# Dummy products of ones at the head of TensorE's program in seven stages of a transformer kernel

## What is computed

```python
x = x + attention0(layernorm(x), ctx, tau, delta)   # softmax attention, 16 heads of 16
x = x + moe0(layernorm(x))        # top 2 of 8 experts, 256-512-256, inner norm + GELU, outer norm
x = x + attention1(layernorm(x), ctx, tau, delta)
x = x + quantum_ffn(layernorm(x)) # 256-1024-256, hidden + c * sin(theta + hidden / 10), relu
x = x + window_attention(ctx, layernorm(x), len, p) # one head, masked, tanh of a projection
x = x + moe2(layernorm(x))        # top 2 of 8 experts, 256-1024-256, GELU
x = x + attention3(layernorm(x), ctx, tau, delta)
x = x + ternary_ffn(layernorm(x)) # rounded activations, weights in {-1, 0, 1}, silu(gate) * up
```

## Time and profile before

| | us |
|---|---|
| median of 3 runs | 2499.39 |
| lowest, highest | 2496.64, 2502.64 |
| profiled execution | 2496.09 |
| its span, first to last instruction | 2494.3 |
| mean granted clock of TensorE, share of full | 0.879 |
| first 40th to last: TensorE's granted clock in tenths | 9997559999955799899989655999999996999699 |

### The profile page before, as it was taken

The page is one execution under the profiler, slowest core; times in us unless marked ns, Lnnn a source line. Parts: engine busy times, 40 slices in busy tenths (PEclk is TensorE's granted clock), DMA queues, the critical chain, the costliest instruction groups (busy, mean ns, idle before and its releaser), DMA issues. The chain is left out here.

```text
span 2494.3 us, 40430 instructions
## 1 busy us (share of the span) xinstructions
PE 1960.8 (79%) x11858; PEld 1467.3 (59%) x11859; DVE 1378.0 (55%) x3378; ACT 894.4 (36%) x1938; POOL 522.7 (21%) x560
## 2 busy tenths in 40 slices
PE   6997419999800699699979751999999994999587
PEld 4665406666500366366666441899999993565255
DVE  5875426666467477778756443222222222787787
ACT  3452104444311344333312110333333332545587
POOL 1212532211187111101100164000000004562000
PEclk9997559999955799899989655999999996999699
DMA  6000231221121400000000323111111113110001
GB/s 243 1 1 22 80 132 57 63 62 61 56 74 58 180 1 1 13 1 0 0 8 10 135 89 108 30 38 34 38 35 36 38 34 121 39 47 1 8 27 35
DMA packets 81874, 125.70 MB, mean 50 GB/s; under 512 B 17104, under 2 KB 65872, under 8 KB 78704
## 3 DMA queue, kind: packets, MB, share of 16 engines
q1 hardware_dynamic: 46640, 68.02, 8.2%
q0 software_dynamic: 13104, 35.80, 4.4%
q10 hardware_dynamic: 22032, 20.62, 2.4%
HBM read 82.58 MB, written 41.81 MB: 50 GB/s over the span
## 5 line engine op out<-in xcount | busy, mean ns | idle before, releaser
L1386 ACT ACTIVATE e_hT<-psum,e_bt 128x128 f32<-128x128 f32 x568 | 154.2, 383 | 335.3 <-PE psum L1349 335.3
L1349 PEld LDWEIGHTS psum<-e_xT,e_w 128*128 128x128 f32 x2272 | 267.0, 193 | 8.4 <-ACT e_xT L1379 4.9
L1349 PE MATMUL psum<-e_xT,e_w 128*128 128x128 f32 x2272 | 267.7, 276 | 4.2 <-ACT e_xT L1379 4.2
L1358 PE MATMUL psum<-m_w,e_hT 128*128 x1136 | 256.8, 379 | 0.0
L268 POOL TENSOR_TENSOR rstd<-lnt,half 128x4 f32<-128x4 f32 (+1 forms) x72 | 75.6, 1050 | 760.9 <-DVE lnt L262 760.8
L1358 PEld LDWEIGHTS psum<-m_w,e_hT 128*128 128x128 f32 x1136 | 210.4, 190 | 25.7
L1414 DVE COPY e_w<-m_w 128x2048 f32 x71 | 87.1, 1227 | 250.0 <-PE psum L1349 224.6
L698 DVE TENSOR_REDUCE a_mx<-psum 128x8 f32<-128x512 f32 x192 | 123.2, 684 | 109.4 <-PE psum L502 109.1
L483 PE MATMUL psum<-a_cx,att_wk 128*128 128x64 f32 x192 | 29.9, 305 | 165.0 <-DMA a_cx<-in_ctxT 165.0
L1212 ACT ACTIVATE e_hT<-psum,e_bt,e_gt 128x128 f32<-128x128 f32 x284 | 106.7, 456 | 140.8 <-PE psum L1175 140.8
L627 ACT ACTIVATE a_pT<-psum 128x512 f32<-128x512 f32 x192 | 104.0, 594 | 127.3 <-PE psum L552 127.2
(11 more groups left out here) (275 smaller groups left out, 3898.4 us busy)
## 6 DMA issues: line engine op xcount, KB each, us to landing
e_x<-sorted_in SPq DMA_DIRECT2D x142, 128.0 KB, 2.2
sorted_out<-e_y ACTq DMA_DIRECT2D x142, 128.0 KB, 1.7
m_w<-in_L_ffn_w SPq DMA_DIRECT2D x16, 1024.0 KB
m_w<-in_L_ffn_w SPq DMA_DIRECT2D x16, 512.0 KB
x_res<-in_x SPq DMA_DIRECT2D x8, 512.0 KB, 7.1
out_x<-x_res SPq DMA_DIRECT2D x8, 512.0 KB, 2.9
a_cx<-in_ctxT SPq DMA_DIRECT2D x40, 64.0 KB, 2.3
e_b<-in_L_ffn_b SPq DMA_DIRECT2D x2, 1024.0 KB, 4.2
```

The costliest lines, as they stand in the source:

```text
L1349: mm = pe.matmul(h_b[s][:, f, :], w1[:, kk, f * P:(f + 1) * P], xT[s][:, kk, :], start=(kk == 0), stop=(kk == DC - 1))
L1358: mm = pe.matmul(y_b[s][:, 0:D], hT[s][:, f, :], k.w2[:, bass.ds(e * (FC * D) + f * D, D)], start=(f == 0), stop=(f == FC - 1))
L1386: g = act.activation(hT[s][:, f, :], h_b[s][:, f, :], ACT.Gelu, bias=bt[:, bass.ds(e * FC + f, 1)])
```

## The change

A function `warm` issues `count` products of `k.ones` with a broadcast of itself, 512 columns wide, into a bank of the block, each with start and stop. It is called once, ahead of the first wait, in TensorE's program of seven blocks: 12 in a0, 64 in a3, none in a1; 64 in the expert block of m0; 8 in that of m2; 10 in f1; 10 in w2; 14 in f3. It waits for nothing and signals nothing. Nothing reads what it writes; the block's own first product into that bank (with start) overwrites it.

```diff
+def warm(pe, k, bank, count):
+
+    for _ in range(count):
+        pe.matmul(bank[:, 0:512].rearrange("p (r l) -> p r l", r=4), k.ones[:, :],
+                  k.ones[:, None, :].to_broadcast([P, 4, P]), start=True, stop=True, skip_group_check=True)
...
@@ attention
+                warm(pe, k, out_b, 12 if loading else 64 if arrival else 0)
                 pe.wait_ge(k.att_in, 16 * k.att_loads)
...
@@ experts
+                warm(pe, k, y_b, 64)
                 pe.wait_ge(k.w_in, k.w_count)
...
@@ experts_gelu
+                warm(pe, k, y_b[0], 8)
                 pe.wait_ge(k.w_in, k.w_count)
...
@@ quantum_ffn
             def _(pe):
+                warm(pe, k, yb[0], 10)
                 pe.wait_ge(w_in, 64)
...
@@ window_attention
             def _(pe):
+                warm(pe, k, tb, 10)
                 pe.wait_ge(w_in, 64)
...
@@ ternary_ffn
+                warm(pe, k, yb, 14)
                 pe.wait_ge(v, 3)
```

## The result

The changed kernel takes **2505.97 us** (median of 9 runs, 2499.04 to 2509.82); the kernel before, run beside it, takes 2498.87 us (9 runs, 2494.89 to 2503.38). The ratio is 1.0025, 95% interval [1.0014, 1.0036]: slower, by more than the 0.2% that such a measurement can tell, where the forecast had 4 us less and a range that ended at 2501.0. The profiled execution after is 2505.97 us with a span of 2504.1, that is 9.8 us longer than the profiled one before.

The account below looks back on a forecast made before the run. TensorE sets the pace or nearly so inside stages (matmuls busy 79% of the span); the change can buy only its clock. 1.6 - 3.6 - 2.0 - 0.3 = -4.3, taken as 4.2: 2499.4 - 4.2 = 2495.2 us, range 2488.5 to 2501.0.

Parts of the forecast that it names:

- Last attention: 64 dummies delay the keys to about 2097.3, done by 2099, before VectorE wants them at 2101.26: no effect.
- The list of what would be wrong: Signs against the forecast: expert burst ending after e_x lands, upper clock behind gaps over 5 us, VectorE waiting for last-attention keys.
- First experts, -3.6: First expert stage: 64 dummies fit the 16.9 us free; transposes and layer 1 run at the upper clock, 3.6 us gained.
- First attention, +1.6: First attention: 12 dummies take 5.2 us where 2.6 us are free, delaying a serial chain: 1.6 us lost.
- the forecast's other case: First attention: if the clock rises inside the burst, the keys' 3.0 us halve and the chain is 0.3 to 1.1 us late.
- Window attention, -2.0 as half of 4.0: Window attention: a 4.3 us burst raises the clock with chance one half, saving 4.0 us: 2.0 us counted.
- R1: Rival, 20%: window attention gains nothing, burst too short or clock falls before the work; -2.0 us in all, 2497.4 us.
- Quantum layer, -0.3: Quantum layer: the clock falls in 2.1 us idle between two sets of transposes; 0.3 us gained, about 2.3 if it held.
- Second experts and ternary layer, nothing: Second expert stage and ternary layer: bursts fit idle time, but the clock falls again before the work: no effect either way.
- R3: Rival, 8%: dummies of ones do not raise the clock; experts and last-attention keys come late, 23 us slower, 2522.6 us.

Follow-up runs that it names:

- e2: Kernel before plus only the 64 dummies of the last attention: 2508.12 us, ratio 1.0035.
- e6: Kernel before plus 64 dummies in the last attention alone, then a TensorE wait for the gathers of tile 2: 2508.76 us, ratio 1.0033.
- e3: Kernel before, no dummies; in the last attention TensorE waits for the third gathered row tile before the keys and values: 2500.63 us, ratio 1.0006.
- e7: Kernel before plus 64 dummies in the last attention alone, with the next weights' transfers held until the gathers of tile 11 landed: 2508.81 us, ratio 1.0037.
- e8: Kernel before plus 64 dummies in the last attention alone, GpSimd's second eight gathers moved behind the second root and first bias addition: 2499.76 us, ratio 1.0000.
- e11: Kernel before plus only the 64 dummies ahead of the first experts: 2493.27 us, ratio 0.9988.
- e1: Changed kernel without the 64 dummies of the last attention, all other dummies kept: 2497.16 us, ratio 0.9993.
- e10: Kernel before plus dummies in three stages alone: 64 in the first experts, 10 in the quantum stage, 14 in the window attention: 2492.27 us, ratio 0.9977.
- e12: Kernel before plus 44 dummies in the last attention alone: 2505.52 us, ratio 1.0032.
- e5: Kernel before plus 64 dummies in the last attention alone, behind the first keys-and-values products instead of ahead: 2502.05 us, ratio 1.0017.
- e13: Kernel before plus 64 dummies of 128 columns instead of 512, in the last attention alone: ratio 1.0006.
- e14: Kernel before plus 14 dummies of f32 ones, 512 columns, in the last attention alone: ratio 1.0003.

## Why the prediction was wrong

**Last attention: "They delay the keys ... That hides the burst ... Nothing."** This is the step that failed, by 11.2 us, more than the whole result. Its times were nearly right: counted from the opening, it had the keys start at 16.4 us and done by 18.1; they started at 15.6 and were done at 20.1, gaps between the value products included, and VectorE was free for them at 20.7. What it took for granted is that a signal sent in time arrives in time. Here TensorE's signal, behind a long burst among GpSimd's gathers, came only when the gathers had ended, and VectorE sat idle for 14.8 us. That was shown by e2 (the dummies alone do it), e6 against e3 (the burst does it, not the place of the keys), e7 (not the weights' transfers) and e8 (take the gathers behind 2101 away and it comes 2.75 us behind the last of the others). By what path it is held is open. The trace of before held a hint: four "remote" waits of VectorE, all where GpSimd issues indirect transfers, in each of which the signal came 2.3 to 3.1 us behind its product. They were not read. The list of what would be wrong did name VectorE waiting for the keys.

**First experts, -3.6.** The mechanism was right: the burst fits, layer 1 runs at the upper clock at once, and the head gained 3.79 us (377.47 to 373.68). That the size fits too is in part luck. In before it is 8.7 us from the start of layer 1 to the transposes of h; in eleven of the fifteen profiles without these dummies only 6.7 to 7.1, and with them 5.3. So the gain is 3.4 us against a head like that of before and some 1.6 against the commoner one, 2.3 us in the mean of the stages. e11's 4.1 us in the medians is compatible with both.

**First attention, +1.6.** Right mechanism, too large: 0.27 by the stage, which is less than its scatter. The clock rose inside the burst, so the keys took 1.00 us instead of 1.94. VectorE's start on them came 5.98 us after the opening instead of 5.73. That is just under the forecast's other case (0.3 to 1.1).

**Window attention, -2.0 as half of 4.0.** The half that fails came: +0.44. R1's place was right, and so was its doubt whether 4.3 us is enough. In e1 the same head failed in R1's other way: its ten dummies ran at the upper clock, in 2.32 us, and after 3.25 us of idle time the transposes took 1.94 us again. In e10 four more dummies were enough, with 5.2 us for the stage, not 4.0: the forecast stopped at the scores, but in before the lower clock lasts through the next transposes and products, to 1305.84.

**Quantum layer, -0.3.** "I expect a fall right there" was wrong in this execution; the head gained about the 2.3 us named for that case, but the stage only 0.88, and in e10, where the clock did fall between the two sets of transposes, nothing.

**Second experts and ternary layer, nothing.** Right: idle times of 5.65 and 4.75 us stand behind the bursts and the work is as slow as before.

Without the last attention the sum is e1: 0.9993 [0.9983, 1.0004], 1.4 us less than before beside it, nearer R1's -2.0 than the forecast's -4.2, and not told from no change. R3 (ones do not raise the clock) was wrong in its premise, though the place it named for its loss, keys late at VectorE in the last attention, is where the loss was.

In the Trainium skill, "TensorE: Matmul & The Clock Gate", section "Part 4: PE-mode transpose", transposes don't bring the upper clock on. The rows don't contradict this, but its use in the forecast was too wide: a clock that is already up is kept across them, in e10 for all the work behind, and in the quantum head of after.

## What to carry to other kernels

Before filling an engine's free time, look who signals whom in it. Here, behind a long run of TensorE instructions beside back-to-back indirect transfers of GpSimd, a signal of TensorE came up to 16 us late, so work that looked free cost 11 us; 24 dummies in the same place cost nothing. A "remote" wait in the profile was the mark of it. A warm-up burst pays where TensorE is the bound right behind it and the gap to the work is short; take a few dummies more rather than a few less, since those behind the rise run at twice the rate (fourteen took 4.87 us, ten at the lower clock 4.43), and drop those with 5 us of idle time behind them.

## What was not expected of the hardware

- TensorE's signals are held back by up to 16.2 us (e12: keys done 11.6 us, seen 27.8 us after the first gather) while the gathers run, and after a burst of 64 its own products are spaced by gaps of 0.5 to 2.6 us, 4.56 in e5, in which it waits for nothing that the profile shows. In the Trainium skill, "SBUF — State Buffer", section "Who interferes with whom", the only contention is that of VectorE and GpSimd for their shared port. That page is on SBUF, and no run here tells what path the signals take, so the two need not conflict; but the rule alone would have let one expect no delay, and TensorE is slowed beside GpSimd's gathers.
- Chips differ in this: on the one where the kernel before takes 2474 us, e13 and e14 have no such wait, each dispatch is 10 us or more shorter, and the dummies cost nothing. e2 itself was not run there.
- The clock rose within ten dummies in one stage (granted 0.58 over the burst's 4.00 us, 1.00 behind it) and not in another (4.43 us, 0.50 throughout), in the same execution.
